# Whole-row unpack, one packing copy per row block and sums three quarters of a block later, in a two-layer graph kernel on one core

## The reference

```python
def _L0_gnn_ref(X, adj, W, b):
    deg = jnp.clip(jnp.sum(adj, axis=1, keepdims=True) + 1.0, 1.0, None)
    h_neigh = (adj @ X + X) / deg
    out = jax.nn.relu(jnp.concatenate([X, h_neigh], axis=1) @ W + b)
    return out / jnp.maximum(jnp.linalg.norm(out, axis=1, keepdims=True), L2_EPS)

def _L1_gnn_ref(features, adj, W):
    neigh = adj @ features / (jnp.sum(adj, axis=1, keepdims=True) + 1.0)
    return jnp.concatenate([features, neigh], axis=-1) @ W.T

x = _layernorm(x + _L0_gnn_ref(x, adj, L0_gnn_W, L0_gnn_b), axis=-1)
x = _layernorm(x + _L1_gnn_ref(x, adj, L1_gnn_W), axis=-1)
```

## Time and profile before

| | us |
|---|---|
| median of 3 runs | 763.99 |
| lowest, highest | 763.28, 767.74 |
| the profiled execution | 763.49 |
| its span in the profile | 761.70 |
| TensorE busy, of the span | 633.2 (83%) |
| VectorE busy | 690.5 (91%) |
| ScalarE busy | 587.2 (77%) |
| POOL busy | 283.8 (37%) |

### The profile page before, as it was taken

One profiled execution on the slowest core, in us unless ns is written; L12 is line 12 of the kernel. 1 busy time (PEld: TensorE's weight loads), 2 busy tenths in 40 slices (PEclk: granted clock), 3 DMA queues, 4 the chain that ended last, 5 costly groups with the idle time before them and its releaser, 6 DMA issues.

```text
span 761.7 us, 27876 instructions
## 1 busy us (share of the span) xinstructions
PE 633.2 (83%) x11125; PEld 581.1 (76%) x11125; DVE 690.5 (91%) x2662; ACT 587.2 (77%) x815; POOL 283.8 (37%) x314
## 2 busy tenths in 40 slices
PE   0346788777778787889799898999999999998994
PEld 0346777676667676778788797989898989988994
DVE  2799987999898999999999999999999999988884
ACT  1978778999888898979889898888898888840032
POOL 0222212543222435345253634463543526331034
PEclk9987766999999999999999999999999999999998
DMA  9999999999999999999999999999999999900003
GB/s 361 384 368 393 421 367 421 421 419 420 418 419 421 416 419 417 404 418 405 421 405 421 405 419 404 419 408 403 404 397 419 409 417 406 411 14 2 3 19 100
DMA packets 41515, 274.53 MB, mean 360 GB/s; under 512 B 4454, under 2 KB 8614, under 8 KB 8614
## 3 DMA queue, kind: packets, MB, share of 16 engines
q1 hardware_dynamic: 39040, 270.55, 87.0%
q10 hardware_dynamic: 2342, 2.16, 0.9%
HBM read 270.60 MB, written 2.10 MB: 358 GB/s over the span
## 4 chain that ended last, share of the span: by engine, by line
PE 27%; DVE 26%; DMA 20%; issue 12%; ACT 9%; POOL 5%; ACTq 0%; DVEq 0%; SPq 0%
DMA a_in<-in_adj 18%; PE s_ps L383 14%; DVE e L792 7%; ACT junk L585 7%; DVE t_sb L799 6%; PE u_ps L402 4%; POOL small L1173 4%; DMA xl<-in_x 2%; DVE q_sb L866 2%; PE z_ps L450 2%; DVE y_sb L860 2%; PE p_ps L369 2%; PE p_ps L462 1%; DVE a_in L799 1%; DVE u_sb L799 1%
## 5 line engine op out<-in xcount | busy, mean ns | idle before, releaser
L585 ACT ACTIVATE junk<-a_in 128x2048 uint8<-128x2048 uint16 x256 | 488.9, 1915 | 10.4 <-DMA a_in<-in_adj 10.2
L383 PE MATMUL s_ps<-xh,t_sb 128*128 128x129 f16 x4096 | 390.2, 252 | 37.5 <-DVE t_sb L799 33.5
L383 PEld LDWEIGHTS s_ps<-xh,t_sb 128*128 128x128 fp8e4 x4096 | 315.3, 103 | 67.7 <-DVE t_sb L799 38.8
L792 DVE TENSOR_SCALAR e<-a_in 128x2048 uint8<-128x2048 f32 x256 | 311.0, 1222 | 12.5 <-DMA a_in<-in_adj 11.5
L1190 POOL COPY store<-pk 128x32 uint32<-128x32 uint32 (+1 forms) x250 | 203.2, 854 | 236.3 <-ACT pk L594 236.3
L799 DVE TENSOR_SCALAR t_sb<-pk 128x128 uint32<-128x128 uint32 x1024 | 152.0, 220 | 3.1 <-ACT pk L594 2.1
L369 PE MATMUL p_ps<-pow_h,e 128*128 128x16 f16 x2048 | 90.8, 171 | 68.8 <-DVE e L792 59.0
L1173 POOL TENSOR_TENSOR small<-small,minus_half 128x4 f32<-128x4 f32 x32 | 70.0, 2187 | 196.8 <-DVE small L854 149.7
L369 PEld LDWEIGHTS p_ps<-pow_h,e 128*128 128x128 f16 x2048 | 77.9, 99 | 83.1 <-DVE e L792 70.2
L402 PE MATMUL u_ps<-xh,u_sb 128*128 128x64 f16 x2976 | 105.6, 192 | 0.0
L402 PEld LDWEIGHTS u_ps<-xh,u_sb 128*128 128x128 fp8e4 x2976 | 100.4, 97 | 1.3
(11 more groups left out here) (119 smaller groups left out, 465.0 us busy)
## 6 DMA issues: line engine op xcount, KB each, us to landing
a_in<-in_adj SPq DMA_DIRECT2D x256, 1024.0 KB, 11.5
xl<-in_x ACTq DMA_DIRECT2D x4, 512.0 KB, 18.3
out_h<-e SPq DMA_DIRECT2D x8, 256.0 KB, 2.2
b_sb<-in_L_gnn_b ACTq DMA_DIRECT2D x3, 0.2 KB
w_sb<-in_L_gnn_W ACTq DMA_DIRECT2D x1, 32.0 KB
w_raw<-in_L_gnn_W ACTq DMA_DIRECT2D x1, 32.0 KB
```

The costliest lines, as they stand in the source:

```text
L383: last = nc.tensor.matmul(s_ps[:, n % 2, at:GW], t_sb[:, b // 2, b % 2::2], xh[:, b, at:GW], start=(b == 0), stop=False)
L585: nc.scalar.activation(junk[:, t % 2, :], halves[t % R], ACT.Copy, scale=1.0 / 128, accum_out=half_sum[:, n, c:c + 1]).then_inc(s_half, 1)
L792: nc.vector.tensor_scalar(e8[:, c, :], a_in[:, t % R, :], 1.0, float(CODE), ALU.is_equal, ALU.add).then_inc(s_e, 1)
```

## The change

- Packing and unpacking go by whole row blocks. p_ps gets one bank per block (n % 2), take_packed copies 512 columns once, t_sb is double and unpack(n) writes 128 x 256 words with eight instructions instead of sixteen of 128 words.
- The sums of a block run three quarters of a block later: the function quarter(n, c) gives quarter 0 of block n - 1 only after the last chunk of block n, and quarters 1 to 3 in the next block. The catch-up moves by one block. transpose_cat moves to k = 2 after the third chunk, dense to just before the fourth chunk, transpose_h to k = 3 after the last chunk, dense_h to k = 0 of the next group. The loops of ScalarE, VectorE and POOL are reordered to match.
- The sums of squares in norm become a Square on ScalarE (after relu) and one reduction. The adds of high and low halves move from VectorE to POOL (join_x, join_g). h_sb is replaced by y_sb, h_t by cat_t.
- Beginning: the four chunks of block 0 are packed before the weights are transposed; splitting x into halves moves from block 0 to block 1; weights and bias both stand in block 2, and guard_x in blocks 3 to 6.
- Epilogue and end: NA is 2 instead of 4; the verdict's copy to bad_i stands before the last add instead of after the last scaling; SyncE reads the verdict before it waits for the stores.

```diff
-        t_sb = sb("t_sb", [P, NB // 2, 2 * P], FP8)
+        t_sb = sb("t_sb", [P, 2, NB // 2, 2 * P], FP8)
...
+        def quarter(n, c):
+
+            return (n - 1, 0) if c == 3 else (n - 2, c + 1)
...
-            for i in range(4):
-                sp.wait_ge(s_out[i], 16 * NV // 4)
...
             if_bad(sp, general_sp)
+            for i in range(4):
+                sp.wait_ge(s_out[i], 16 * NV // 4)
...
-                if c % 2 == 0 and n:
-                    pe.wait_ge(s_pk, (n - 1) * 2 + c // 2 + 1)
+                if c == 0 and n >= 2:
+                    pe.wait_ge(s_pk, n - 1)
                 for u in range(CB // 2):
-                    at = ((c % 2) * CB // 2 + u) * PK
-                    last = nc.tensor.matmul(p_ps[:, c // 2, at:at + PK], e_pair[:, c, u // 2, :, u % 2],
+                    at = (c * CB // 2 + u) * PK
+                    last = nc.tensor.matmul(p_ps[:, n % 2, at:at + PK], e_pair[:, c, u // 2, :, u % 2],
                                             pow_h[:, :], start=True, stop=True)
                 last.then_inc(s_pps, 1)
...
-                    pe.wait_ge(s_t, n * 2 + i // 2 + 1)
+                if i == 0:
+                    pe.wait_ge(s_t, n + 1)
...
+                if n + 1 < NB and n + 1 == START[seg(n + 1)] and n and i * CB < lows(n):
+                    pe.wait_ge(s_glo, min(lows(n), (i + 1) * CB) // BR)
...
-                    last = nc.tensor.matmul(s_ps[:, n % 2, at:GW], t_sb[:, b // 2, b % 2::2], xh[:, b, at:GW],
+                    last = nc.tensor.matmul(s_ps[:, n % 2, at:GW], t_sb[:, n % 2, b // 2, b % 2::2], xh[:, b, at:GW],
...
-                if i % 2:
                     last.then_inc(s_sum, 1)
...
+                    if n == START[q]:
+                        pe.wait_ge(s_glo, low(q) // BR)
...
+            for c in range(NC):
+                pack_chunk(0, c)
...
+            for n in range(1, NB):
                 e, k = n // BR - 1, n % BR
-                if e >= 0 and k == 2:
-                    dense(e)
                 for c in range(NC):
+                    if e >= 0 and (k, c) == (2, 3):
+                        dense(e)
                     pack_chunk(n, c)
-                    if e >= 0 and (k, c) == (1, 3):
+                    if e >= 1 and (k, c) == (0, 1):
+                        dense_h(e - 1)
+                    if n > 1 or c == 3:
+                        sum_quarter(*quarter(n, c))
+                    if n > START[1] and c < 2:
+                        catch_up(n - 1, c)
+                    if e >= 0 and (k, c) == (2, 2):
                         transpose_cat(e)
-                    if n == START[seg(n)] and n and c == 0:
-                        pe.wait_ge(s_glo, low(seg(n)) // BR)
-                    if n:
-                        sum_quarter(n - 1, c)
-                    if e >= 0 and (k, c) == (3, 0):
+                    if e >= 0 and (k, c) == (3, 3):
                         transpose_h(e)
-                    if n >= START[1] and c in (1, 2):
-                        catch_up(n, c - 1)
-                    if e >= 0 and (k, c) == (3, 1):
-                        dense_h(e)
             e = NE - 1
+            sum_quarter(NB - 2, 1)
+            dense_h(e - 1)
+            catch_up(NB - 1, 0)
+            sum_quarter(NB - 2, 2)
+            catch_up(NB - 1, 1)
+            sum_quarter(NB - 2, 3)
             for c in range(NC):
                 sum_quarter(NB - 1, c)
             pe.wait_ge(s_agg, NB)
...
                 act.wait_ge(s_in[t % R], 16 * (t // R + 1))
-                if t >= 2:
-                    act.wait_ge(s_half, t - 1)
-                nc.scalar.activation(junk[:, t % 2, :], halves[t % R], ACT.Copy, scale=1.0 / 128,
+                if t:
+                    act.wait_ge(s_half, t)
+                nc.scalar.activation(junk[:, :], halves[t % R], ACT.Copy, scale=1.0 / 128,
                                      accum_out=half_sum[:, n, c:c + 1]).then_inc(s_half, 1)
-            def take_packed(n, h):
...
-                act.wait_ge(s_pps, n * NC + 2 * h + 2)
+            def take_packed(n):
+
+                act.wait_ge(s_pps, (n + 1) * NC)
                 if n >= 2:
-                    act.wait_ge(s_t, (n - 2) * 2 + h + 1)
+                    act.wait_ge(s_t, n - 1)
                     act.wait_ge(s_store, n - 1)
-                nc.scalar.activation(pk_u[:, n % 2, h * 256:(h + 1) * 256], p_ps[:, h, 0:256], ACT.Copy,
+                nc.scalar.activation(pk_u[:, n % 2, :], p_ps[:, n % 2, :], ACT.Copy,
                                      bias=-CODE_SUM, scale=1024.0).then_inc(s_pk, 1)
             def take_sums(n):
                 e, k = n // BR, n % BR
-                act.wait_ge(s_sum, n * 2 + 2)
...
                         nc.scalar.activation(r_sb[:, :, :].rearrange("p k i -> p (k i)"), z_flat[:, 0:BR * F],
                                              ACT.Copy if layer else ACT.Relu).then_inc(g_z, 1)
-            act.wait_ge(s_w1t, 1)
-            nc.scalar.copy(w1_sb[:, :], c_ps[:, 0, 0:F])
-            nc.scalar.copy(w2_sb[:, 0:F], c_ps[0:F, 2, 0:F])
-            nc.scalar.copy(w2_sb[:, F:2 * F], c_ps[0:F, 1, 0:F]).then_inc(s_w1, 1)
+            def take_weights():
+
+                act.wait_ge(s_w1t, 1)
+                nc.scalar.copy(w1_sb[:, :], c_ps[:, 0, 0:F])
+                nc.scalar.copy(w2_sb[:, 0:F], c_ps[0:F, 2, 0:F])
+                nc.scalar.copy(w2_sb[:, F:2 * F], c_ps[0:F, 1, 0:F]).then_inc(s_w1, 1)
             for n in range(NB):
                 e, k = n // BR - 1, n % BR
                 sum_codes(n, 0)
+                if e >= 1 and k == 0:
+                    take_h(e - 1)
+                if n:
+                    take_packed(n - 1)
+                if n == 1:
+                    split_x(0)
+                sum_codes(n, 1)
+                if n == 1:
+                    split_x(1)
+                if e >= 1 and k == 0:
+                    take_g(e - 1)
+                sum_codes(n, 2)
+                if n == 1:
+                    split_x(2)
+                if e >= 0 and k == 2:
+                    take_cat(e)
+                sum_codes(n, 3)
+                if n == 1:
+                    split_x(3)
+                    take_weights()
+                if n >= 2:
+                    take_sums(n - 2)
                 if e >= 0 and k == 2:
                     take_z(e)
-                if n == 0:
-                    split_x(0)
-                sum_codes(n, 1)
-                if n == 0:
-                    split_x(1)
-                if n:
-                    take_packed(n - 1, 1)
-                if n >= 2:
-                    take_sums(n - 2)
-                if e >= 0 and k == 3:
-                    take_h(e)
-                sum_codes(n, 2)
-                if n == 0:
-                    split_x(2)
-                take_packed(n, 0)
-                if e >= 0 and k == 3:
-                    take_g(e)
-                sum_codes(n, 3)
-                if n == 0:
-                    split_x(3)
-                if e >= 0 and k == 1:
-                    take_cat(e)
             e = NE - 1
-            take_packed(NB - 1, 1)
+            take_h(e - 1)
+            take_packed(NB - 1)
+            take_g(e - 1)
             take_sums(NB - 2)
             take_sums(NB - 1)
...
-                if n:
-                    dve.wait_ge(s_sum, (n - 1) * 2 + h + 1)
-                half = slice(h * NB // 4, (h + 1) * NB // 4)
-                dst = words(t_sb[:, half, :])
+            def unpack(n):
+
+                dve.wait_ge(s_pk, n + 1)
+                if n >= 2:
+                    dve.wait_ge(s_sum, n - 1)
+                dst = words(t_sb[:, n % 2, :, :])
                 unpack_planes(lambda g: dst[:, :, g * 2 * PKW:(g + 1) * 2 * PKW],
-                              pk_w[:, n % 2, :].rearrange("p (u w) -> p u w", w=2 * PKW)[:, half, :]).then_inc(s_t, 1)
+                              pk_w[:, n % 2, :].rearrange("p (u w) -> p u w", w=2 * PKW)).then_inc(s_t, 1)
             def unpack_piece(n):
...
-                link(nc.vector.reciprocal(small[:, 0, :], dcol[:, rows]))
-                link(nc.vector.tensor_tensor(s_sb[:, :, :], agg[:, par, :, HP:HP + F], agg[:, par, :, HP + F:2 * HP],
-                                             ALU.add))
+                link(nc.vector.reciprocal(small[:, 0, :], agg[:, par, :, 2 * HP:GW].rearrange("p k o -> p (k o)")))
+                dve.wait_ge(s_xsum, e + 1)
                 if e:
                     dve.wait_ge(s_catps, e)
-                nc.vector.tensor_tensor(cat_in[:, :, F:2 * F], s_sb[:, :, :], bc(small[:, 0, :], BR),
+                nc.vector.tensor_tensor(cat_in[:, :, F:2 * F], agg[:, par, :, HP:HP + F], bc(small[:, 0, :], BR),
                                         ALU.mult).then_inc(s_mean, 1)
...
-                    ins = nc.vector.scalar_tensor_tensor(out=q_sb[:, k, :], in0=r_sb[:, k, :], scalar=1.0,
```

(98 more changed lines are left out.)

70 lines of the change are left out of this document (35 added, 35 removed).

## The result

The changed kernel takes 770.74 us (median; 769.50 to 771.87) against 764.0 for the kernel before, a ratio of 1.0092 with the interval 1.0081 to 1.0103: 7 us slower, where I had forecast 2 us faster. Its span is 768.8 us.

What follows compares the result with a forecast made beforehand. Up to block 44 loads, start and VectorE set the pace, then TensorE. From 763.5 us: arrival -12.6, backlog +7.0, new waits +8.0, tail -3.5, making 762.4, stated as 762; range 749 to 771 us.

Steps and rivals of the forecast that it cites:

- the second rival: Start: weights, bias and guard keep VectorE behind until block 8; gain at block 44 only 5 to 6 us; chance 0.08.
- Arrival at block 44: First packing of block 44 at 459.5 us instead of 472.1: gain 12.6 us, bounds 8 and 17.
- an arrival later than 465: Block 44: the prediction called itself wrong if the arrival there came later than 465 us.
- From there to the last product it is TensorE.: From block 44 to the last product at 750.65 us, TensorE sets the pace; 10.2 us a block counted, 10.4 measured.
- Backlog and waits: TensorE from block 44: later sums, catch-up and dense_h give back 7.0 us; new waits, net of today's idle, add 8.0.
- a cat copy wait: Between transpose_cat and dense, TensorE waits for ScalarE's copy of cat_t: 0.75 us, five times, 3.8 us.
- chunk 3's: Chain after dense: TensorE reaches chunk 3's packing at 12.9, VectorE's compare ends at 13.3, a stall of 0.4 us.
- the pair behind it: After chunk 3's packing: VectorE's work to the next compare takes 3.6 us, TensorE's 2.5, another 1.2 us per group.
- The tail: Epilogue and end: last add directly after the last product, -0.95 us; earlier TensorE branch, 2.5 us; together -3.5 us.
- TensorE stays fed: From block 44: VectorE's saved 1 us per block keeps a lead, giving 755 us, or 752 with earlier arrival; chance 0.36.
- POOL late: join_x on POOL takes up to 6.27 us, putting 13 us on TensorE's path, 775 us; chance 0.12.
- hidden: POOL's join_x before mean costs nothing, as it can start over 2 us before mean.

Runs made afterwards that it cites:

- b_half: The kernel before, leaving out the products with the low half of the features in the catch-up from block 44 on: 761.91 us (0.9980).
- a_cat: The changed kernel with transpose_cat moved ahead of the quarter of sums at k = 2, c = 2: 765.97 us (1.0028).
- a_lag2_cat: a_cat with the sums half a block late instead of three quarters, and the unpack ahead of the third compare: 763.60 us (1.0008).
- a_junk2: The changed kernel with a second buffer for the code sums' thrown-away output given back: 769.66 us (1.0078).
- a_lag2_cat_junk2: The changed kernel with transpose_cat ahead of the quarter of sums, half a block of lag and two buffers for the code sums' output: 763.37 us (0.9998).
- b_start: The kernel before with only the changed kernel's beginning (block 0 packed before the weights are transposed, splits of x in block 1): 764.66 us (1.0017).

## Why the prediction was wrong, point by point

The sum was 763.5 - 12.6 + 7.0 + 8.0 - 3.5. With what the traces show, it is 763.5 - 5.7 + 13.8 - 1.0 = 770.6, and the profiled execution took 770.70. What came is the number of the second rival, "the beginning gives little", 769 to 770, which had 0.08. That it fits is mostly luck. VectorE was behind the landings until about chunk 38 (12.0 us at chunk 12), much as the rival says, but this explains at most 1.4 us of the 6.9 that were missing at block 44.

**Arrival at block 44, 12.6 forecast, 5.7 measured: the step that failed.** I took the moment at which the queue would have moved 188.9 MB (458.2 us), added 1.3 us for compare and handover, and called that the first packing of block 44. (188.9 MB are 177 chunks with x and instructions, so chunk 176 is in it.) From this I subtracted a packing that was measured. Chunk 176 before, then after: its load, its compare (the first of the three in the changed kernel's row) and its packing.

```profile
455.54 0.33 SPq L331 DMA_DIRECT2D a_in<-in_adj  x1
a_in<-in_adj SPq DMA_DIRECT2D x1, 1024.0 KB, 12.8
470.82 1.21 DVE L792 TENSOR_SCALAR e<-a_in 128x2048 uint8<-128x2048 f32 x1
472.09 0.36 PE L369 MATMUL p_ps<-pow_h,e 128*128 128x16 f16 x8
```

```profile
450.32 0.33 SPq L335 DMA_DIRECT2D a_in<-in_adj  x1
a_in<-in_adj SPq DMA_DIRECT2D x1, 1024.0 KB, 11.1
465.11 3.49 DVE L812 TENSOR_SCALAR e<-a_in 128x2048 uint8<-128x2048 f32 x3
466.38 0.36 PE L372 MATMUL p_ps<-pow_h,e 128*128 128x16 f16 x8 [0.51 <-DVE e L812]
```

| us | before | changed | forecast for the changed kernel |
|---|---|---|---|
| 188.9 MB moved, at the mean rates of 408 and 411 GB/s | 463.0 | 459.6 | 458.2 |
| chunk 176 landed | 468.3 | 461.5 | taken as the same moment |
| compared | 470.8 | 465.1 | |
| packed | 472.1 | 466.4 | 459.5 |

The bytes came nearly as forecast, 1.4 us late. What failed is the term of 1.3 us from them to the packing: it measured 6.8 us in the changed kernel, and 9.1 in the kernel before. Some 11 to 13 us pass from issue to landing, so four or five loads are under way at once, and parts of the later ones have moved when chunk 176 is complete; that is 1.9 us here and 5.3 before (by 468.3 us, 408 GB/s less 3.2 MB make 179 chunks' worth, and 177 had landed). Then the chunk waits for VectorE, which in the changed kernel has the compare of chunk 175, add_piece, unpack_piece and normalise ahead of it, 3.7 us. The forecast compared an early event of the new kernel with a late one of the old. My own sign of being wrong, an arrival later than 465, came true.

By the rate alone the claim would have been 5 us: at 408 GB/s the kernel before was 470.5 x 11/419 = 12.4 us short of 419 GB/s, and the forecast itself left 7.4 us of that in. The 408 GB/s stood in the earlier trace rows, beside the count that I used. The measured rates say the same: 367 us x (417 - 413)/417 = 3.5 us, and 100 x (393 - 387)/417 = 1.4 us at the start, 4.9 together.

**"From there to the last product it is TensorE."** This step also fell, for the kernel before. 98% busy and my count of 10.2 us a block against 10.4 measured seemed to prove it; b_half removes 24 us (16 after the fall of the clock) and gains 1.1, and the landings of the kernel before keep the loads' pace to the end. 10.4 us a block was the loads' pace too (four chunks at 2.57 are 10.3), and a product's recorded time had covered the waits. What b_half doesn't touch is the work behind the last packing, and there the lag is paid. That three resources were full within some per cent should have been read as three candidates.

**Backlog and waits: +15.0 forecast, +13.8 measured,** from the first packing of block 44 (466.4) to the last product's end (758.77), 292.4 against 278.6 us. Of these, 3.8 us come up to the last packing, 9.9 between it and the first product of the tail (18.0 for 8.1), 0.2 in the tail. The places and sizes of the waits held: a cat copy wait of 0.68 for 0.75, chunk 3's of 0.44 for 0.4, the pair behind it 0.79 for 1.2. a_cat (4.8) and a_lag2_cat (2.4 for a quarter of 1.8) confirm both by removal, and a_junk2 adds up to 1.1 that I hadn't counted. These three make 8.3 by the single edits; stacked, the last product starts at 753.9, 752.0 and 751.0, which is 7.6 of the 8.1 us. That the total comes so near is luck in part: it was counted against a TensorE that paced the kernel before, and it didn't.

**The tail: -3.5 forecast, -1.0 measured** (10.1 us from the last product's end to the span's end, for 11.05). Neither half gave what I had put down for it:

```profile
757.39 0.68 DVE L938 TENSOR_TENSOR xl<-s_ps,xl 128x512 f32<-128x512 f32 x1
...
758.11 0.63 ACT L661 ACTIVATE t_sb<-xl 128x512 f32<-128x512 f32 x1 [2.16 <-DVE xl L938]
758.77 0.69 DVE L948 TENSOR_REDUCE fvar<-t_sb 128x8 f32<-128x512 f32 x1 [0.70 <-ACT t_sb L661]
...
760.25 0.67 DVE L938 TENSOR_TENSOR xl<-u_ps,xl 128x512 f32<-128x512 f32 x1
```

The last add stands 1.5 us behind the product, not 0.1. The epilogue had become a ring of add, square on ScalarE, reduction, scale and again add. Its adds follow each other by 2.79 us (751.81, 754.60, 757.39); the groups of products are 3.8 us apart, so it was catching up on a lateness and hadn't at the end, and VectorE's program has the previous group's reduction and scale ahead of the last add. The branch did start earlier relative to the last add, and the store decided, as forecast (by line; min/median/max ns, first to last start):

```profile
L320 PEldq COMPARE_BRANCH  x1: 3971/3971/3971, 761.2 to 761.2; - x1
...
L319 SPq TENSOR_LOAD <-bad_i x1: 476/476/476, 765.7 to 765.7; - x1
...
L361 SPq EVENT_SEMAPHORE  x2: 17/22/28, 766.7 to 768.4; - x2
```

The last store is issued at 765.3, and SyncE's wait for it ends at 768.4: 3.1 us from issue to landing, where I had taken the 2.1 of the kernel before. The late add (1.4 us) and the slower landing (1.0) are the 2.5 us that were missing.

**The other rivals.** TensorE stays fed (0.36): no, VectorE is at 86% and still late for chunk 3 in each group, because it waits for ScalarE's Square, as argued. POOL late (0.12): its time didn't come, but its mechanism is there, and "hidden" was wrong. The wait counter puts only 0.7 us of the whole run down to join_x, because it puts most of these waits down to VectorE's own reciprocal; the timeline shows more.

```profile
612.87 2.75 POOL L1194 TENSOR_TENSOR agg<-agg 128x256 f32<-128x256 f32 x1 [2.83 <-ACT agg L618]
614.95 0.17 DVE L856 RECIPROCAL small<-agg 128x4 f32<-128x4 f32 x1
615.71 0.43 DVE L860 TENSOR_TENSOR cat_in<-agg,small 128x256 f32<-128x256 f32 x1 [0.59 <-DVE small L856]
```

The reciprocal named there had ended at 615.12; cat_in starts 0.1 us after join_x ends at 615.62. VectorE stands so in each of the five groups after 467 us, four times 0.6 us and once 0.9, 3.3 us in all, where I had put nothing; join_x takes 2.7 to 3.0 us there, against 0.73 at its shortest. TensorE's transposes of cat_in record no wait in these groups, so no cost of it on the path is shown.

**Why the repaired kernel ends no earlier.** The table of landings answers it. In a_lag2_cat_junk2 the last chunk lands 7.6 us earlier than in the kernel before and is packed 7.7 us earlier. But between that packing and the tail stand 16.2 us of TensorE's work instead of 8.1: two more quarters of sums, transposes, dense_h and catch-up, all of which the kernel before has done by then. The change buys 7.7 us at the loads and pays them back behind the last chunk.

**What stays open.** What the whole-row unpack is worth by itself, and whether the lag can be drained over the last blocks, so that less stands behind the last packing; neither was run. The changed kernel leads by 4.3 us when chunk 40 lands (116.0 instead of 120.3), and b_start didn't bring that; which part does wasn't separated.
